# Score product in 64x64 parts, and an unused table corner filled in the first step alone, in a chunked delta-rule attention loop

## The reference, cut to what matters

```python
def step(S, xs):
    q_t, k_t, v_t, g_t, b_t = xs
    S = S * jnp.exp(g_t)[..., None, None]
    kv = jnp.einsum('bhk,bhkv->bhv', k_t, S)
    S = S + jnp.einsum('bhk,bhv->bhkv', k_t, (v_t - kv) * b_t[..., None])
    o_t = jnp.einsum('bhk,bhkv->bhv', q_t, S)
    return (S, o_t)
```

## Time and profile before

| | |
|---|---|
| median of 3 runs | 4280.13 us |
| the profiled execution's own time | 4290.22 us |
| its span | 4288.5 us |
| PE busy | 3741.9 us (87%) |
| VectorE busy | 2212.2 us (52%) |
| ScalarE busy | 1375.6 us (32%) |
| GpSimd busy | 882.5 us (21%) |
| mean granted TensorE clock | 0.943 |

### The profile page before, as it was taken

One profiled execution on the slowest core, in us unless ns is written; L12 is line 12 of the kernel. 1 busy time (PEld: TensorE's weight loads), 2 busy tenths in 40 slices (PEclk: granted clock), 3 DMA queues, 4 the chain that ended last, 5 costly groups with the idle time before them and its releaser, 6 DMA issues. The chain is left out here.

```text
span 4288.5 us, 83786 instructions
## 1 busy us (share of the span) xinstructions
PE 3741.9 (87%) x34608; PEld 2300.2 (54%) x34608; DVE 2212.2 (52%) x4555; ACT 1375.6 (32%) x2456; POOL 882.5 (21%) x1248
## 2 busy tenths in 40 slices
PE   6988898899798879889979888988997988898898
PEld 4873344465487434446548733444655964353555
DVE  5755434554565453455457555345536745444543
ACT  4422222432443222244144222225314431312431
POOL 2620101130153010113026201012202620101220
PEclk9989899989899999999989999999999989999999
DMA  2001000010000100000000010000100001000000
GB/s 88 3 13 51 21 3 17 25 39 28 27 3 13 51 21 1 20 25 39 28 28 3 13 51 21 17 3 25 39 28 28 3 12 51 21 19 1 25 39 30
DMA packets 10940, 104.24 MB, mean 24 GB/s; under 512 B 1148, under 2 KB 5552, under 8 KB 6192
## 3 DMA queue, kind: packets, MB, share of 16 engines
q1 hardware_dynamic: 10544, 98.69, 6.0%
HBM read 97.64 MB, written 1.05 MB: 23 GB/s over the span
## 5 line engine op out<-in xcount | busy, mean ns | idle before, releaser
L89 PE MATMUL psum<-ident_bf 128*128 128x512 bf16 x2012 | 536.2, 404 | 148.1 <-DVE l_attn_peak L913 57.5
L89 PEld LDWEIGHTS psum<-ident_bf 128*128 128x128 bf16 x2012 | 194.9, 103 | 398.7 <-issue 140.6
L496 DVE TENSOR_TENSOR l_ffn_hidden<-l_ffn_silu,psum 128x512 f32<-128x512 f32 (+2 forms) x176 | 120.8, 687 | 319.1 <-ACT l_ffn_silu L435 319.1
L95 PEld LDWEIGHTS psum<-streamed_weights,l_ffn_hidden 128*128 128x128 f32 (+1 forms) x1664 | 215.1, 191 | 115.1 <-issue 102.9
L435 ACT ACTIVATE l_ffn_silu<-psum 128x512 f32<-128x512 f32 (+1 forms) x208 | 124.1, 597 | 470.5 <-PE psum L404 416.8
L2825 PE MATMUL psum<-l_attn_xx,l_attn_part 64*64 64x64 f32 x5120 | 236.7, 225 | 27.5 <-DVE l_attn_xx L3237 19.0
L151 POOL TENSOR_TENSOR norm_rstd<-norm_var,minus_half 128x2 f32<-128x2 f32 x104 | 75.2, 723 | 884.9 <-DVE norm_var L164 884.5
L3032 ACT ACTIVATE l_attn_ax<-psum 128x256 f32<-128x256 f32 x320 | 122.2, 383 | 387.5 <-PE psum L2825 377.5
L913 DVE TENSOR_REDUCE l_attn_peak<-psum 128x4 f32<-128x2048 f32 (+3 forms) x128 | 185.7, 1486 | 95.5 <-PE psum L808 94.9
L2825 PEld LDWEIGHTS psum<-l_attn_xx,l_attn_part 64*64 64x64 f32 x5120 | 205.9, 136 | 48.9 <-DVE l_attn_xx L3237 23.4
L95 PE MATMUL psum<-streamed_weights,l_ffn_hidden 128*128 128x128 f32 (+1 forms) x1664 | 223.6, 277 | 9.2 <-DVE l_ffn_hidden L493 5.0
(11 more groups left out here) (538 smaller groups left out, 7975.4 us busy)
## 6 DMA issues: line engine op xcount, KB each, us to landing
streamed_weights<-pack_l_ffn SPq DMA_DIRECT2D x4, 5284.0 KB, 15.5
streamed_weights<-pack_l_ffn SPq DMA_DIRECT2D x4, 3972.0 KB, 12.5
streamed_weights<-pack_l_attn SPq DMA_DIRECT2D x5, 2848.5 KB, 9.8
streamed_weights<-pack_l_xattn SPq DMA_DIRECT2D x4, 2496.0 KB, 9.0
streamed_weights<-pack_l_ffn SPq DMA_DIRECT2D x4, 2192.0 KB, 8.0
streamed_weights<-pack_l_xattn SPq DMA_DIRECT2D x4, 2048.0 KB, 7.5
streamed_weights<-pack_l_ffn SPq DMA_DIRECT2D x4, 1923.0 KB, 8.0
streamed_weights<-pack_l_attn SPq DMA_DIRECT2D x4, 1107.5 KB, 5.0
```

What stands on the lines that cost most here:

```text
L89: pe.matmul(self.bank(bank), self.ident_bf[:, :], self.ident_bf[:, :].unsqueeze(1).to_broadcast([P, NT, P]), start=True, stop=True)
L95: ins = pe.matmul(self.psum[:, OUT, t * P:(t + 1) * P], features[:, t * P:(t + 1) * P], weight, start=first and t == 0, stop=last, skip_gr ...
L496: dve.tensor_tensor(hidden[0:r, n % 2, :], silu[0:r, n % 2, :], m.bank(2 + n % 2)[0:r], ALU.mult).then_inc(hidden_ready, 1)
```

## The change

It is in two functions of PE's list; no other engine's code, no buffer and no semaphore changes.

In `prep`, the two matmuls that fill the corner (`LOW`, columns 64 to 127, of the decays and of the products) are now issued in step 0 alone. From step 1 on a prep has 4 matmuls instead of 6, and the corner keeps what step 0 of the pass left in the bank. The order within a half is now lower block first, then upper block, and the semaphore comes with the last upper one.

In `output_first`, each product of 64 rows by 128 columns is issued as two of 64 by 64, one for each half of the output's partitions (16 matmuls instead of 8). Both read `pm[TOP]` and the same `u_[TOP]`.

```diff
-                    for lo in (W, 0):
-                        pe.matmul(bank[LOW, 2:4, W - lo:P - lo], m.const["after"][:, W:P], gu[:, p % 2, :, lo:lo + W],
-                                  start=True, stop=True)
-                        if lo:
-                            pe.matmul(bank[TOP, 2:4, :], m.const["after"][:, 0:W], gu[:, p % 2, :, :], start=True, stop=True)
-                    for lo in (W, 0):
-                        ins = pe.matmul(bank[LOW, 0:2, W - lo:P - lo], qk[rows, 0, f, mid_:mid_ + W],
-                                        qk[rows, 0:2, f, at + lo:at + lo + W], start=True, stop=True)
-                        if lo:
-                            pe.matmul(bank[TOP, 0:2, :], qk[rows, 0, f, at:mid_], qk[rows, 0:2, f, tok(t)], start=True,
-                                      stop=True)
-                    ins.then_inc(prep_psum, 1)
+                    pe.matmul(bank[LOW, 2:4, 0:W], m.const["after"][:, W:P], gu[:, p % 2, :, W:P], start=True, stop=True)
+                    if n == 0:
+                        pe.matmul(bank[LOW, 2:4, W:P], m.const["after"][:, W:P], gu[:, p % 2, :, 0:W], start=True, stop=True)
+                    pe.matmul(bank[TOP, 2:4, :], m.const["after"][:, 0:W], gu[:, p % 2, :, :], start=True, stop=True)
+                    pe.matmul(bank[LOW, 0:2, 0:W], qk[rows, 0, f, mid_:mid_ + W], qk[rows, 0:2, f, mid_:mid_ + W], start=True,
+                              stop=True)
+                    if n == 0:
+                        pe.matmul(bank[LOW, 0:2, W:P], qk[rows, 0, f, mid_:mid_ + W], qk[rows, 0:2, f, at:mid_], start=True,
+                                  stop=True)
+                    pe.matmul(bank[TOP, 0:2, :], qk[rows, 0, f, at:mid_], qk[rows, 0:2, f, tok(t)], start=True,
+                              stop=True).then_inc(prep_psum, 1)
...
                     for p in range(4):
                         for i in range(2):
-                            ins = pe.matmul(m.psum[:, 6 + p % 2, column(p, i, 1)], pm[TOP, n % 3, p, i, :], u_[TOP, p, i, :],
-                                            start=p < 2 and i == 0, stop=True, skip_group_check=True)
+                            for b in BLOCKS:
+                                ins = pe.matmul(m.psum[b, 6 + p % 2, column(p, i, 1)], pm[TOP, n % 3, p, i, b],
+                                                u_[TOP, p, i, :], start=p < 2 and i == 0, stop=True, skip_group_check=True)
                     ins.then_inc(pu1_psum, 1)
```

## The result

The changed kernel takes 4246.6 us (median of 20 runs, 4216.3 to 4284.84), the kernel before 4284.01 in the 20 runs beside it. The ratio is 0.9917, 95% interval 0.99 to 0.9933: 0.83% faster, 37.4 us by the medians. The forecast was 4244. One of the 20 runs of the kernel before took 8813 us, and two of the changed kernel's (4284.84 and 4279.88, at a mean clock of 0.931) count as slow too; the ratio leaves the slow runs out.

What follows compares the result with a forecast made beforehand. PE was taken to bound the loop, apart from one VectorE-bound wait at each step's start. Savings of 30 us (score product) and 6 us (preps) off the 4280.13 us median gave 4244 us, range 4230 to 4272.

Steps and rivals of the forecast that it cites:

- What bounds the loop: Steady loop step of 21.68 us: a PE stream with one VectorE-bound wait; PE time saved at levels 1 to 4 counts.
- the notch: PE's 0.37 us idle at a step's start, waiting for begin's end; time saved just ahead turns into idle there.
- Part 1, the price: Score product as 32 records of 64x64: 34 ns each, 1.09 us against 1.93, 0.84 us less a step.
- the third: Trace evidence from L1901: column halves reading the same rows run side by side, four record starts within 0.06 us.
- the serial rival: Score product's column halves serialise at one block's pace, 58 ns a record: 4271 us; chance 0.09.
- The slow seven: Score products outside the 25 steady ones, partly at low clock: 20.7 us in all, expected to save 9.3.
- Part 1, the cover: After the score product, VectorE's X of level 3 is ready 0.96 us before PE needs it, so no wait.
- Part 2: Two of six prep matmuls dropped from step 1: 0.11 us in each of 56 odd preps, 6 us.
- one visible interval, the one that is certain: Odd preps' score half: lower block free 0.11 us earlier, taken from a possible 0.11 to 0.22.
- The sum: Whole kernel: 30 us plus 6 us, 36 us off the median of 4280.13, giving 4244.
- the slower one: Score product: loads of one row group don't overlap its matmuls, 108 ns a record, 4328 us; chance 0.04.

Runs made afterwards that it cites:

- halves_apart: Changed kernel with the score product's 16 matmuls reordered, all eight of the upper column half first, then the lower; one run, 4277.65 us.
- padded: Changed kernel with 50 more filler matmuls of 512 columns ahead of the first prep; ratio 0.999 to the kernel before.

## Why the prediction was right, and where it was not

**What bounds the loop**: right. Every edit of PE's time at levels 1 to 4 came off the step to 0.03 us (0.85, 0.44, 1.28, 0.70), and the notch stayed, 0.38 us. That time saved ahead of the notch would be lost was not tested: the only work taken away there is that of p = 0's prep, and an even prep gave nothing anywhere.

**Part 1, the price**: right, to the 10 ns. 34 ns a record, 1.08 us against the 1.09 taken, shared rows or not. The row that carried it was the third, L1901, whose pairs start within 0.06 us; halves_apart confirms the mechanism, and also shows how near the serial rival was: in an order that keeps to one block, 57 ns a record, the gain of 0.85 us is 0.11. The slow seven gained 11 us where I took 9.3 (70.7 - 38.4 = 32.3, less 25 x 0.85). In part that is the draw of the clock: in the changed kernel's trace five of the seven take 1.15 us, as at full clock, and two 1.98 and 1.97.

**Part 1, the cover**: right. No wait took the gain, and 0.70 us more came through.

**Part 2**: the mechanism and the places were right (score corner only, odd preps only), the term was mis-sized: 0.22 us, not 0.11. The step that failed is the choice of "one visible interval, the one that is certain" out of the two that the block lost. L2806's block lost two records of 0.11, and what follows moved up by both (`second_rows` starts 1.78 us behind the prep's first record, 166.97 to 168.75, where it was 2.00, 171.00 to 173.00); that the upper block still streams does not hold it up. 12 us instead of 6.

**The sum**: 36 us predicted, 44 at equal clock, 37.4 by the medians. That the prediction hit the medians is luck, because two errors of opposite sign met: the loop gained 8 us more than the sum, and the stages behind gave back 7 to 16 (more, if the loops of the traces are taken) that it had no term for. A small part of that follows from the definition (44 us at clock 1.00 taken out of a mean of 0.945 lowers it by 0.0006, some 2 us). The rest is, by the traces, time spent at a lower clock in stages with unchanged instructions.

**The rivals**: the slower one is out: L2891 at 34 ns instead of the 60 from which it decides. The Trainium skill (TensorE: Matmul & The Clock Gate, Part 3, on what overlaps) lets a load overlap running matmuls only across row groups; by it halves that share 64 rows don't overlap, and by the rows of the slower rival that would have been 108 ns a record. Both the 34 ns of the alternating order and the 57 ns of the single block, where a load record alone is 135 ns long, speak against it, and the measurement decides. The Trainium skill (the same page, TensorE: Matmul & The Clock Gate, Part 3) also states that matmuls start in program order; here L2824's first record, at 167.56 (in program order behind all of the prep's), starts ahead of L2804's second (167.71 in the timeline above), so the measurement decides there too.

**Left open**: why the later stages' clock is lower behind a shorter loop. The mean clocks (0.9414 and 0.9397 changed, 0.9462 padded, 0.9451 to 0.9453 before) point to when these stages start; the one trace of the padded kernel does not bear it out, and it isn't settled. That it is this, and not the loop, that took back a part of the gain rests on the equal-clock comparison and on the stages' times in single traces.

## What to carry to other kernels

Here the pace of matmuls with 64 moving columns went with the columns of their weights (121 ns a record for 128, 57 for 64 on one block). Splitting such a matmul into column halves pays if neighbours in the list alternate between the halves, and hardly if each half is done in one run. In a packed array look for the block whose stream ends last: taking work from another one is free of effect, as the decays' corner was. And where the granted clock moves, compare kernels at equal mean clock too: here the medians showed 28 to 37 of some 44 us.

## What the runs showed of the hardware that I had not expected

A run's time follows its mean granted clock closely (2.9 us per 0.001 over 79 runs), and kernels with equal instructions behind the loop seem to differ in it: a stage of equal instructions took 83.8 or 87.1 us. Matmuls whose result nobody reads, put where PE waits 0.7 to 2.7 us, kept the clock at 1.00 for the whole tail, though they do no work; in that trace each pass's loop was 3 to 12 us shorter than in the changed kernel's.
